# Score and exponent products in four 32-row tiles of TensorE instead of two 64-row tiles, with three split products a head

## What is computed

```
scores = einsum('bhqd,bhkd->bhqk', Qh, Kh)          # 8 features a head
scores = (scores + einsum('bhqd,qkd->bhqk', Qh, rel_k)) / sqrt(8)
scores = where(causal, scores, -1e9)
attn   = softmax(scores)
out    = einsum('bhqk,bhkd->bhqd', attn, Vh) + ...
```

## Time and profile before

| | us |
|---|---|
| median of three runs | 1034.78 |
| lowest and highest run | 1034.72, 1037.62 |
| the profiled execution, first to last instruction | 1036.5 |
| PE busy (matmul) | 896.3 (86%) |
| VectorE (DVE) busy | 833.7 (80%) |
| POOL busy | 727.1 (70%) |
| ScalarE (ACT) busy | 676.3 (65%) |

### The profile page before, as it was taken

The page is one execution under the profiler, slowest core; times in us unless marked ns, Lnnn a source line. Parts: engine busy times, 40 slices in busy tenths (PEclk is TensorE's granted clock), DMA queues, the critical chain, the costliest instruction groups (busy, mean ns, idle before and its releaser), DMA issues. The chain is left out here.

```text
span 1036.5 us, 23477 instructions
## 1 busy us (share of the span) xinstructions
PE 896.3 (86%) x7655; PEld 513.6 (50%) x7655; DVE 833.7 (80%) x1948; ACT 676.3 (65%) x1305; POOL 727.1 (70%) x940
## 2 busy tenths in 40 slices
PE   2778889889889898898898988986679999999995
PEld 0324444444444444444444444432457777777773
DVE  5578888888988888889888888877568788878884
ACT  2038677777676777776777777765447767676773
POOL 4135686876867868768678687576357989898886
PEclk9769999999999999999999999988889999999999
DMA  2610110110101101011011011101425455555441
GB/s 48 170 44 34 35 44 31 47 42 32 49 31 42 45 32 47 32 43 49 32 42 44 33 47 40 35 18 50 148 59 169 144 165 150 169 151 166 162 140 31
DMA packets 64004, 74.93 MB, mean 72 GB/s; under 512 B 10032, under 2 KB 39600, under 8 KB 63904
## 3 DMA queue, kind: packets, MB, share of 16 engines
q1 hardware_dynamic: 61536, 73.17, 22.4%
q10 hardware_dynamic: 2368, 0.48, 0.3%
HBM read 43.75 MB, written 8.65 MB: 51 GB/s over the span
## 5 line engine op out<-in xcount | busy, mean ns | idle before, releaser
L1128 DVE TENSOR_REDUCE mx<-ps_s 128x1 f32<-128x512 f32 (+2 forms) x640 | 408.6, 681 | 84.3 <-PE ps_s L1540 83.7
L799 ACT ACTIVATE prob<-ps_e 128x512 f32<-128x512 f32 x640 | 349.6, 606 | 103.3 <-PE ps_e L1497 103.2
L641 POOL TENSOR_SCALAR_AFFINE_SELECT prob<-prob 128x516 f32<-128x516 f32 (+1 forms) x320 | 174.9, 571 | 141.8 <-ACT prob L799 141.8
L1519 PE MATMUL ps_s<-ks,qs 63*128 63x512 f16 (+3 forms) x1024 | 224.5, 312 | 47.4 <-DVE mx L1128 31.5
L1497 PE MATMUL ps_e<-qs,ks 64*128 64x512 f16 (+3 forms) x1024 | 212.1, 307 | 3.7 <-ACT prob L799 1.7
L721 POOL TENSOR_TENSOR hidden_low<-hidden,hidden_high 128x512 fp32r<-128x512 f32 x144 | 191.1, 1356 | 12.1 <-ACT hidden_high L989 10.9
L1557 PE MATMUL ps_av<-prob,vp 128*32 128x512 f32 (+3 forms) x2048 | 182.4, 452 | 4.3 <-POOL prob L641 4.2
L1519 PEld LDWEIGHTS ps_s<-ks,qs 63*128 63x128 f16 x1024 | 67.6, 95 | 184.0 <-DVE mx L1128 80.5
L989 ACT CAST hidden_high<-hidden 128x512 fp32r<-128x512 f32 x160 | 98.0, 612 | 30.5 <-DVE hidden L1441 27.3
L1540 PE MATMUL ps_s<-masked_at,below_r 64*128 64x128 bf16 (+3 forms) x640 | 103.1, 211 | 0.0
L1540 PE MATMUL ps_s<-masked_at,below 64*128 64x128 bf16 (+3 forms) x640 | 91.3, 213 | 0.0
(11 more groups left out here) (177 smaller groups left out, 1737.7 us busy)
## 6 DMA issues: line engine op xcount, KB each, us to landing
gate_rows<-gates_dram SPq DMA_DIRECT2D x128, 256.0 KB, 3.6
qs<-qh SPq DMA_DIRECT2D x128, 32.0 KB
qs<-ql SPq DMA_DIRECT2D x128, 32.0 KB
xnT_dram<-oT SPq DMA_DIRECT2D x16, 256.0 KB, 2.0
xeT<-xnT_dram SPq DMA_DIRECT2D x16, 256.0 KB, 2.7
out<-result SPq DMA_DIRECT2D x16, 256.0 KB, 2.3
v_near<-v_back SPq DMA_DIRECT2D x16, 254.0 KB
ks<-kh SPq DMA_DIRECT2D x124, 32.0 KB
```

The lines of the kernel that those rows point to most:

```text
L641: pool.affine_select(out=v, in_=v, compare_op=ALU.is_ge, fill=0.0, base=-2, pattern=cols, channel_multiplier=-1).then_inc(S["p_masked"], 1)
L799: act.activation(prob[g % 2][:, u, b, :], ps_e[bank][:, :], ACT.Exp, scale=SCALE).then_inc(S["e_done"], 1)
L1128: dve.tensor_reduce(out, src, AX.X, ALU.max).then_inc(s_free[bank], 1)
L1519: pe.matmul(scores[:, at:at + P * (qt + 1)], qs[par][rows, 2 * g + off, P * qt:P * qt + P], ks[par][rows, 2 * g + off, 0:P * (qt + 1)], st ...
```

## The change

- A head takes three products, high by high, high by low and low by high, as 24 rows; with the row of the maxima they fit in 32 rows, one of four row tiles of the array.
- The stacks become [128 partitions, 4 slots, 512 tokens]: the four heads of a group of even number lie in partitions 0 to 63 (two row tiles, two slots), those of an odd group in 64 to 127. The rows of the three products are interleaved (row 4d+r of a tile is product r of feature d).
- Stage A goes through the groups in the order 1, 0, 3, 2, stage B in 0, 1, 2, 3. So the four banks of a round, two of stage A and two of stage B, use four different row tiles. Order of issue, banks, rings and rounds stay.
- The causal mask remains a product with 64 rows. Both heads of stage A now lie in the same row half as the mask's rows, so the four mask matmuls of a round all use the same half; they are issued head by head.
- `stacks_out` has 3 DMAs of 64 KB for `qs` and 3 for `ks` for a sequence and a half, `first_keys` 3 instead of 8. The buffers `qs` and `ks` are half as large, and a spare buffer keeps the others where they were.
- The constant column of `ks` has four rows to set instead of two, in a chain on POOL.

```diff
+S_GROUP = [1, 0, 3, 2]
+def quad(g, b):
+    return slice(QUAD * (2 * (g % 2) + b), QUAD * (2 * (g % 2) + b) + QUAD)
+def slot(g, off):
+    return 2 * (g // 2) + off
...
-                for stk, parts in ((qs[par], (qh, qh, ql, ql)), (ks[par], (kh, kl, kh, kl))):
+                for stk, parts in ((qs[par], (qh, qh, ql)), (ks[par], (kh, kl, kh))):
...
-                    for b in range(2):
-                        for r, part in enumerate(parts):
-                            lo = 64 * b + D * r
-                            src = 64 * b + 32 * half
-                            sp.dma_start(stk[lo:lo + D, prs, :], part[src:src + 32, :]).then_inc(stacks[par][half], 16)
+                    for r, part in enumerate(parts):
+                        sp.dma_start(stk[r:P:4, slots, :], part[rows, :]).then_inc(stacks[par][half], 16)
...
-                    row = HALF * b + M_ROW
-                    sp.dma_start(qs[s % 2][row:row + 1, 4 * half:4 * half + 4, :],
+                    row = QUAD * b + M_ROW
+                    sp.dma_start(qs[s % 2][row:P:2 * QUAD, 2 * half:2 * half + 2, :],
...
-            pool.affine_select(out=m_col[:, :], in_=m_col[:, :], compare_op=ALU.not_equal, fill=-M_UNIT,
-                               base=-M_ROW, pattern=[[0, 2]], channel_multiplier=1).then_inc(S["m_made"], 1)
-            pool.wait_ge(S["m_made"], 1)
-            pool.affine_select(out=m_col[:, :], in_=m_col[:, :], compare_op=ALU.not_equal, fill=-M_UNIT,
-                               base=-M_ROW - HALF, pattern=[[0, 2]], channel_multiplier=1).then_inc(S["const_ready"], 1)
+            for c in range(4):
+                done = S["m_made"] if c < 3 else S["const_ready"]
+                pool.affine_select(out=m_col[:, :], in_=m_col[:, :], compare_op=ALU.not_equal, fill=-M_UNIT,
+                                   base=-M_ROW - QUAD * c, pattern=[[0, 2]], channel_multiplier=1).then_inc(done, 1)
+                if c < 3:
+                    pool.wait_ge(S["m_made"], c + 1)
...
-                for b in range(2):
-                    for r, part in enumerate((kh, kl, kh, kl)):
-                        lo = HALF * b + D * r
-                        act.dma_start(ks0[lo:lo + D, 0:NPAIR // 2, :],
-                                      part[HALF * b:HALF * b + 32, :]).then_inc(stacks[0][0], 16)
+                for r, part in enumerate((kh, kl, kh)):
+                    act.dma_start(ks0[r:P:4, 0:NSLOT // 2, :], part[0:64, :]).then_inc(stacks[0][0], 16)
...
             def e_part(st, i, scores, n):
-                par, rows = st.b % 2, slice(HALF * b, HALF * b + HALF)
+                par, rows = st.b % 2, quad(g, b)
-                pr = 2 * g + off
+                pr = slot(g, off)
...
             def s_part(st, i, scores, n):
-                par, rows = st.a % 2, slice(HALF * b, HALF * b + M_ROW)
+                first_row = quad(S_GROUP[g], b).start
+                par, rows = st.a % 2, slice(first_row, first_row + M_ROW)
+                pr = slot(S_GROUP[g], off)
...
-            def s_masks(u, both):
-                n = len(S_UNITS[u])
-                for part in range(2):
-                    for b in (1, 0):
-                        rows = slice(HALF * b, HALF * b + HALF)
+            def s_masks(g, u, both):
+                n, half = len(S_UNITS[u]), g % 2
+                rows = slice(HALF * half, HALF * half + HALF)
+                for b in (1, 0):
+                    for part in range(2):
                         columns = masked_at[rows, 0:HALF + part].unsqueeze(1).to_broadcast([HALF, n, HALF + part])
-                        last = pe.matmul(diagonals(both[b], u, part), (below if b == part else below_r)[rows, :],
+                        last = pe.matmul(diagonals(both[b], u, part), (below if half == part else below_r)[rows, :],
                                          columns, start=False, stop=(part == 1))
```

More of the change, by code:

```diff
@@ L20 @@
 NPAIR, NGRP = H // 2, H // 4
+NSLOT = H // 4
 SCALE = float(D) ** -0.5
@@ L24 @@
 MASKED = -1e30
-HALF = P // 2
-M_ROW = HALF - 1
+HALF, QUAD = P // 2, P // 4
+M_ROW = QUAD - 1
 NE, HR, HS = 8, 128, 256
@@ L346, in sb_attention @@
                 return attention.enter_context(nc.sbuf_tensor(name, shape, dt))
-            qs0 = sb_attention("qs0", [P, NPAIR, SEQ], F16)
-            ks0 = sb_attention("ks0", [P, NPAIR, SEQ], F16)
-            sb_attention("apart", [P, NPAIR, SEQ], F16)
+            qs0 = sb_attention("qs0", [P, NSLOT, SEQ], F16)
+            ks0 = sb_attention("ks0", [P, NSLOT, SEQ], F16)
+            sb_attention("apart", [P, 2 * NPAIR, SEQ], F16)
             prob = [sb_attention(f"prob{i}", [P, NU, 2, SEQ]) for i in range(2)]
-            qs1 = sb_attention("qs1", [P, NPAIR, SEQ], F16)
-            ks1 = sb_attention("ks1", [P, NPAIR, SEQ], F16)
+            qs1 = sb_attention("qs1", [P, NSLOT, SEQ], F16)
+            ks1 = sb_attention("ks1", [P, NSLOT, SEQ], F16)
             qs, ks = [qs0, qs1], [ks0, ks1]
@@ L408, in split_heads @@
         def split_heads(v):
-            return v.rearrange("(hf p4 b d) -> b hf d p4", hf=2, b=2, d=D)
+            return v.rearrange("(x off b d) -> x b d off", off=2, b=2, d=D)
         passed = {n: S["passed_" + n] for n in ("sp", "pool", "dve", "pe")}
@@ L426, in _ @@
                 for c in range(4):
-                    load(dst[32 * c:32 * c + 32, :], split_heads(src)[c // 2, c % 2])
+                    load(dst[32 * c:32 * c + 32, :], split_heads(src)[c])
             sp.dma_start(xr[:, 1, :].rearrange("p (i d) -> p i d", i=NT), x_v[:, 1]).then_inc(x_loaded[1], 16)
@@ L441, in stacks_out @@
             def stacks_out(st, s, half):
-                par, prs = s % 2, slice(4 * half, 4 * half + 4)
+                par, slots, rows = s % 2, slice(2 * half, 2 * half + 2), slice(64 * half, 64 * half + 64)
                 if s < 2:
@@ L584, in _ @@
                                pattern=[[-1, P]], channel_multiplier=1).then_inc(S["const_ready"], 1)
[L586 to L589, removed]
+            for off in range(2):
+                v = head_sel[:, :, off:NPAIR:2, :]
+                pool.affine_select(out=v, in_=v, compare_op=ALU.not_equal, fill=1.0, base=-off,
+                                   pattern=[[-2, D], [-32, NPAIR // 2], [-16, 2]],
                                    channel_multiplier=1).then_inc(S["const_ready"], 1)
-            pool.affine_select(out=m_col[:, :], in_=m_col[:, :], compare_op=ALU.not_equal, fill=-M_UNIT,
-                               base=-M_ROW, pattern=[[0, 2]], channel_multiplier=1).then_inc(S["m_made"], 1)
-            pool.wait_ge(S["m_made"], 1)
-            pool.affine_select(out=m_col[:, :], in_=m_col[:, :], compare_op=ALU.not_equal, fill=-M_UNIT,
-                               base=-M_ROW - HALF, pattern=[[0, 2]], channel_multiplier=1).then_inc(S["const_ready"], 1)
+            for c in range(4):
[4 more added lines that the diff above has]
+                    pool.wait_ge(S["m_made"], c + 1)
             def masked_columns():
@@ L819, in q_out @@
                     for half in range(2):
-                        act.wait_ge(stacks[(st.f - 1) % 2][half], st.at(256 * ((st.f - 1) // 2 + 1), 128))
+                        act.wait_ge(stacks[(st.f - 1) % 2][half], st.at(96 * ((st.f - 1) // 2 + 1), 48))
                 act.activation(qh[:, :], ps_e[bank][:, :], ACT.Identity, bias=bq[:, :])
@@ L1047, in qk_constants @@
                         ready(dve.tensor_copy(
-                            dst[:, 64 * b:64 * b + 64].rearrange("p (hf d p4) -> p hf d p4", hf=2, d=D),
-                            src[:, :].rearrange("p (hf p4 b d) -> p b hf d p4", hf=2, b=2, d=D)[:, b]))
+                            dst[:, :].rearrange("p (x b d off) -> p b x d off", b=2, d=D, off=2)[:, b],
+                            src[:, :].rearrange("p (x off b d) -> p b x d off", off=2, b=2, d=D)[:, b]))
                 own.mark(dve.tensor_reduce(feature[:, :], head_sel[:, :, :, :].rearrange("p d pr b -> p d (pr b)"),
@@ L1118, in s_max @@
                 scores, (off, qt, _) = ps_s[bank][:, :], S_UNITS[u][0]
-                h = 2 * (2 * g + off) + b
+                h = 2 * (2 * S_GROUP[g] + off) + b
                 if len(S_UNITS[u]) == 1:
@@ L1505, in s_unit @@
                 if i % HALF_UNITS == 0:
-                    pe.wait_ge(stacks[par][i // HALF_UNITS], st.at(256 * (st.a // 2 + 1), 128))
+                    pe.wait_ge(stacks[par][i // HALF_UNITS], st.at(96 * (st.a // 2 + 1), 48))
                 if i == 0 and st.a < 2:
@@ L1516, in s_part @@
                 g, u, b = i // (2 * NU), i % (2 * NU) // 2, 1 - i % 2
-                par, rows = st.a % 2, slice(HALF * b, HALF * b + M_ROW)
+                first_row = quad(S_GROUP[g], b).start
+                par, rows = st.a % 2, slice(first_row, first_row + M_ROW)
                 off, qt, at = S_UNITS[u][n]
-                pe.matmul(scores[:, at:at + P * (qt + 1)], qs[par][rows, 2 * g + off, P * qt:P * qt + P],
```

(6 more changed lines are left out.)

2 lines of the change are left out of this document (1 added, 1 removed).

## The result

The changed kernel takes 1057.92 us (median of 4 runs, 1054.91 to 1058.54) against 1036.20 for the kernel before in the same session. The ratio of the runs is 1.019, 95% interval 1.0172 to 1.0208: it is slower by 1.9%, outside the forecast range of 1024 to 1051. Its profiled execution spans 1053.2 us, 16.7 more than the one of before. By the medians the difference is 21.7. The profiled execution is the fastest of the four (1054.91), so what follows explains 16.7 us, and 5.0 us of the medians' difference stay unexplained.

What follows compares the result with a forecast made beforehand. Neither PE nor VectorE was full; the pace changed hands within a step, with PE on the path in eight of 20 rounds. Steady state +4, fill -4 and clock +1 us on 1034.8 gave 1036, range 1024 to 1051.

Steps and rivals of the forecast that it cites:

- The clock: Steady stretch: shorter streaming with more gaps leaves PE less active; 1 us added, bounds 0 and 6.
- The stall as cover: Rounds 0, 1, 11 to 17, 4, 5 and 9: PE's changes covered by later stalls, otherwise another 1 us.
- Steady state without the clock: 14 steady steps: path rounds +0.2 us, VectorE's loop up to 0.1; +0.3 us a step, +4 us in all.
- 512 columns: Rounds u = 0 and 3: products -0.22, masks +0.07, switch +0.09, so -0.06 us of PE a round.
- 384 and 128: Rounds u = 1 and 4: products -0.055, masks +0.12, switch +0.09, so +0.16 us of PE a round.
- 256: Round u = 2: products -0.11, masks +0.12, switch +0.09, so +0.10 us of PE a round.
- The masks: Four masks in one row half run serially: +0.07 us in rounds u = 0 and 3, +0.12 in the others.
- the switch: From 32 to 64 rows between products and masks, once a round: 0.09 us empty, bounds 0 and twice that.
- the gain of the products: Four products streaming together save 0.22 us (512 columns), 0.055 (384 and 128) or 0.11 (256) a round.
- rival 1: The four products don't stream together: +1.1 us a step, +15 in all, 1051 us; chance 0.12.
- The fill: Start: fewer DMAs gain 4 and up to 7 us, half-clock loop costs 3; net -4, from -9 to +1.
- Rival 2: Slower by switch (0.18 us) and serial masks, VectorE idling: +17, 1053 us; smaller forms 1041; chance 0.23 with these.

Runs made afterwards that it cites:

- e5: Changed kernel plus 4 filler products of 512 columns in the stall of round 16 of each step: 1044.54 us.
- e7: Kernel of e1 (masks as two pairs) with the round 16 filler of e5: 1030.35 us.
- e8: Kernel of e4 (masks in four 32-row pieces) with 5 filler products in round 16: 1017.50 us.
- e3: Changed kernel with every stage B product of 512 columns issued twice: 1062.03 us.
- e4: Changed kernel with the mask in four 32-row pieces in the row tile of its own head, no switch inside a round: 1030.53 us.
- e2: Changed kernel plus filler products before two other waits, 4 before the normalised input and 3 before the second norm: 1075.86 us.
- e1: Changed kernel with the four masks of a round issued again as two pairs in the two row halves: 1038.91 us.

## Why the prediction was wrong

- **The clock** is the step that failed: "Shorter streaming with more gaps between leaves PE less active in a step; I add 1 us, bounds 0 and 6." The direction was right, the term was mis-sized by more than ten times. In the steady stretch the mean step is 42.67 us, and 41.36 where e5 kept the clock up: 1.31 us a step, 14.4 us in 11 steps, and that covers the whole of the 13.1 us lost there. Against the kernel before, which loses 0.06 us a step to its own falls, it is 13.8. I took the share of time at the low clock as a small average. What decides is where it lies and how long it lasts. Against 41.36, steps of the changed kernel with a fall at 24.1 us take 0.5 more, at 16.4 us 0.9, at 15.6 us 1.4, and those with 6.8 us at the low clock from 15.1 us on 2.5. The slow stretch then lies on the part of the step (from round 16 on) where PE sets the pace.
- **The stall as cover.** I let PE's savings and losses in rounds 11 to 16 vanish into the stalls at no price. Their time was covered, as expected, but 9 of 11 steps paid afterwards, at the low clock. That filler in the stall of round 16 takes those falls away is shown (9 of 11 steps to none in e5, 5 to none in e7, 9 to none in e8). That they came because the stall grew from 0.83 to 1.22 us is not: e3 has them with 0.60. What else changed in that stretch, and makes the clock fall, stays open.
- **Steady state without the clock: +0.3 us a step forecast, -0.06 measured** (41.36 against 41.42). Of the terms, 512 columns held (-0.06 forecast, -0.05 measured). The others were too high: 384 and 128 had +0.16, 256 had +0.10, and both measured +0.01 where PE waits for no bank. The masks cost the 0.12 that I had there, and the switch 0.11 instead of 0.09. Mis-sized was the gain of the products: in all three kinds of round the four stream together and save 0.22 us, where I had 0.055 and 0.11. By these terms the sum for a step is -0.3 us instead of +1.2. What the rounds that wait for a bank add to the path wasn't measured apart.
- **Four row tiles** stream at the full rate of each, so rival 1 is out: in e4, where no switch follows them, the masks start 0.23 us after the first of four products of 512 columns, as the next pair did 0.22 us after the first in the earlier trace rows. The 3.07 of the Trainium skill ("TensorE: Matmul & The Clock Gate", Part 3) for four row tiles is not what this case shows, where the rate is four times that of one. By the rule of the Trainium skill that a change of mode drains the array ("TensorEngine Tiling (Array Packing)", Key Properties) each round had to lose something at the switch; the trace agrees, with 0.11 us.
- **The fill: -4 us forecast, -0.5 measured.** The terms written down (4, up to 7, less 3) didn't add up to 4 without a choice that isn't given. The gains were larger than I counted: the first scores 7.8 us earlier, where 4 was forecast, and step 2 earlier by 5.2. The loss in the loop at 1.2 GHz was as forecast, 0.16 to 0.21 us a round. What I left out is how long the low clock lasts: durations stay at the slow level until about 85 us, while before the record has 2.4 GHz from 75.6 on. From the queries of step 1 to those of step 2 takes 44.9 us against 40.5. With the same fill it took 45.4 in e5 and 45.7 in e3, 43.3 in e2; with paired masks 41.4 (e1) and 42.4 (e7).
- **Rival 2** named the serial masks and gave 1053, near the result, but for another reason: the switch wasn't 0.18, and VectorE's loop isn't what stretched the steps. What serial masks cost shows with the clock equal: steps without a fall last 41.36 us with them (e5) and 40.83 without (e7), 0.53 a step, 7 to 8 us in 14 steps. The medians of e5 and e7 differ by 14.2; how the rest divides between falls, fill and end wasn't separated.
- **From the last steady step to the end +4.0 us** was not forecast. 3.6 of it lie ahead of the last product with the values, where 34 us pass at the low clock instead of 20. With the filler of e5 the stretch to the end takes 411.9 us, but with that of e7 415.7, as in e1 (415.0). That the clock causes the 4.0 is argued, not shown.

## What to carry to other kernels

Work taken from TensorE in a stretch that another engine bounds need not be free even where its time is covered. Here the clock then fell behind that stretch, and the next one, which PE bounds, ran at half speed. So look for PE's long stalls in each period and for the granted clock behind them, and price the stretch that follows at 1.2 GHz before calling the saving or the cover free. The length of a stall alone didn't tell where the clock would fall. The cheapest trial is filler of the stall's length in that one place: it gave this kernel 11 to 13 us, while filler in other stalls cost 18.

And compare a round with the same round. PE can wait for a bank without a stall in the profile, when other products keep it busy; a median over such rounds mixes the cost of the instructions with the pace of the other engine.

## What the runs showed of the hardware

- Four matmuls in 32-row tiles, each with 128 columns of output in its own bank, start within 0.02 us and take no longer than two (0.38 to 0.39 us for 512 columns; what follows in the same tiles starts 0.23 us after them in e4).
- PE going from 32-row to 64-row tiles leaves 0.10 to 0.11 us empty (masks 0.33 us after the first product); masks in the row tile of their product (e4) start after 0.23 us.
- In the changed kernel the clock fell in 9 of 11 steps within 1.4 us behind a stall of 1.22 us, in none of them with that stall filled down to 0.25 us (e5), and in none of the kernel before (0.68 us, with 0.15 ahead of it). But it fell there in 9 of 11 steps with a stall of 0.60 us (e3). Other falls, at 22 to 26 us of a step, follow stalls of 0.33 to 0.94 us.
- The record of the granted clock can lack its beginning: the view says 1.00 where 512 columns take 0.60 us, and the first entry begins at 85.0 us.
